# End of the attention in a two-layer cross-attention kernel: last group's sums in the score banks, transposes ahead of the picks, heads 0 and 1 mostly split beforehand

## Chip, cores and metric

One core of a Trainium2 chip. The metric is the device time of one execution in microseconds, as the median of several. TensorE is PE in the profile, VectorE DVE, ScalarE ACT, GpSimd POOL, SyncE SP.

## What is computed

Two cross-attention layers and an MLP, in float32, on x of 8 x 56 x 256 with one context of 8 x 1500 x 256:

```python
B, Q, D, H, K, T, F = 8, 56, 256, 16, 128, 1500, 1024
def cross(q_in, kv, wq, bq, wk, bk, wv, bv, wo, bo, bias_k, bias_v):
    qh = heads(q_in @ wq + bq)                     # b q h k
    kh = concat(heads(kv @ wk + bk), bias_k)       # one extra key
    vh = concat(heads(kv @ wv + bv), bias_v)       # one extra value
    w  = softmax(einsum('bqhk,bthk->bhqt', qh, kh) / sqrt(K))
    return einsum('bhqt,bthk->bqhk', w, vh).reshape(B, Q, H * K) @ wo + bo
for layer in (1, 2):
    x = x + cross(layer_norm(x), ctx, ...)
x = x + gelu(layer_norm(x) @ w_fc1 + b_fc1) @ w_fc2 + b_fc2
```

## The kernel before

**Order of the mathematics.** Keys and values are never formed. The queries of each head are carried through the head's key weights, so that scores are products with the raw context, and the attention weights multiply the raw context as well. The sum, 256 wide for each of the 8 x 56 x 16 = 7168 rows, is then taken through the value weights and the output weights of its head. The extra key and value come in separately: a column of logits `lb`, its softmax share `pn_extra`, and a product with the row `dv80`.

**Precision.** Each operand is split in two float32r parts, HI (rounded) and LO (the rest), and a product is three matmuls, HI HI, HI LO and LO HI. ACT or VectorE makes HI, VectorE or GpSimd makes LO.

**Attention loop.** A batch has 7 tiles of 128 rows (16 heads times 8 queries each), in two groups of GT = 4 and 3 tiles. A group takes NCT = 12 chunks of 125 context positions. TensorE computes a chunk's scores in one of two score banks (0 and 1, `S_BANK`), ACT copies them to `slots`, VectorE keeps the running maximum. 14 steps later (`SUB_LAG`) VectorE subtracts the maximum (L1142), ACT writes the exponential's HI part in the ring `pt` and again its full value (L893, L894) and GpSimd the LO part (L486); 17 steps later (`PV_LAG`) TensorE multiplies with the context (`weighted_context`, L642 to L644: three matmuls for each tile, 9 for a chunk of the second group) in banks 2 to 5 (`O_BANK`).

**Closing a group.** `normalized`: VectorE forms the denominators and reciprocals (L1177, L1180), ACT scales tiles 0 and 2 (L900), VectorE tile 1 and 3 (L1184) and the extra share (L1186). TensorE transposes `on` into bank 7 (L653) in two goes, and ACT copies each to `qt` (L907), the second go after the first copy. All this normally lies inside the next group's steps.

**The end of a layer**, `batch_steps(B, False, True)`, has no scores any more: 17 steps of lagging work. Then, on TensorE: the 16 picks (L811, which gather `pn_extra` by head in bank 6), the transposes of the last group, and head 0. Each head has these steps: ACT gathers its rows of `qt` as HI (`context_hi`, L954), VectorE the LO part (`context_lo`, L1222); TensorE multiplies with the value weights, six matmuls (L591), and adds `dv80` times `pm` (L666), where `pm` is the picked share times a mask (GpSimd, `mask_extra`, L545); ACT adds the bias and splits off HI (L959), VectorE LO (L1228); TensorE adds the head's output rows (L675, 12 matmuls) in four banks, two heads behind. Weights of the heads are loaded by SyncE in four staging tiles, split by ACT (HI, `weight_hi`, L840) and GpSimd (LO, `weight_lo`, L427); a staging tile is loaded anew after its LO part is done.

**What sets the order.** Every engine's order is written by hand and runs strictly as written; engines wait on counting semaphores. Before the change, of the second weights' first four tiles ACT splits two within the last steps (k = 11 and 13) and two after the picks' copy (L942); GpSimd takes two LO parts at its steps 12 and 13, waits for the last context matmul, makes `dv80` (L531, L534), then the other two LO parts, then `pm` for heads 0 and 1. ACT's order after the last scaled copy is: `p80` (picks), two weights, two transposed copies, then heads 0 and 1. VectorE's is: LO part of the picks (L1233), `context_lo` of heads 0 and 1.

Buffers share space: `w` and `w_raw` lie over the first group's `slots`, `cs`, `pm` and `dv80` over the second's, `oth` (the gathered heads) over the scaled queries `qs`.

## Time and profile before

| | us |
|---|---|
| median of 3 runs | 1302.52 |
| lowest, highest | 1300.93, 1304.53 |
| the profiled execution, its own time | 1303.02 |
| its span in the profile | 1301.2 |
| TensorE busy in the span | 1245.8 (96%) |
| VectorE, ACT, GpSimd busy | 795.3, 806.5, 902.6 |

The busy time of an engine counts its instructions, not waits on semaphores. A row of the timeline is one instruction or a run of like ones, with its start, its duration, and in brackets how long the engine had been idle before it and which operation released it. Matmuls overlap each other, so that rows of 0.28 us start 0.12 us apart. "Granted clock" is TensorE's clock as a share of 2.4 GHz, at either 1.0 or 0.5; values between them are means over a window.

### The profile page before, as it was taken

How to read it: one execution, taken by the hardware profiler on the slowest of the kernel's cores; microseconds unless marked ns; L12 is line 12 of the kernel's file. 1: busy time of each engine (PE TensorE's matmuls, PEld its weight loads, DVE VectorE, ACT ScalarE, POOL GpSimd, SP SyncE). 2: the span in 40 equal slices, each digit the busy share in tenths (PEclk: the TensorE clock that was granted, in tenths of full speed). 3: DMA queues.
4: the chain of work that ended last, by engine and by line, in shares of the span. 5: the costliest groups of instructions: out<-in, count | busy, mean ns of one | idle time of the engine just before them, and what ended most of it. 6: DMA issues, size and time to landing. Idle time of an engine off the chain costs nothing.

```text
span 1301.2 us, 27136 instructions
## 1 busy us (share of the span) xinstructions
PE 1245.8 (96%) x8016; PEld 1144.4 (88%) x8016; DVE 795.3 (61%) x1368; ACT 806.5 (62%) x1572; POOL 902.6 (69%) x750
## 2 busy tenths in 40 slices
PE   6999999999999999989699999999999999999887
PEld 5779999999999998978686999999999999999787
DVE  6855666666666666537684666666656666664554
ACT  4745666666666666666384666666666666667554
POOL 4737777777777686667572768686868786867772
PEclk9999999999999999999899999999999999999898
DMA  5401111111111111122251111111111111101231
GB/s 174 130 9 48 37 60 37 57 43 59 49 50 47 47 47 35 36 59 64 80 165 36 37 36 60 35 59 38 56 45 61 36 59 35 59 24 45 57 90 31
DMA packets 30426, 72.69 MB, mean 56 GB/s; under 512 B 3072, under 2 KB 4144, under 8 KB 30368
## 3 DMA queue, kind: packets, MB, share of 16 engines
q1 hardware_dynamic: 30368, 72.01, 18.0%
q8 instruction: 25, 0.41, 0.1%
q14 instruction: 33, 0.27, 0.1%
HBM read 71.52 MB, written 0.48 MB: 55 GB/s over the span
## 4 chain that ended last, share of the span: by engine, by line
PE 85%; DVE 5%; ACT 3%; issue 3%; DMA 1%; POOL 1%; DVEq 0%; ACTq 0%; POOLq 0%; SPq 0%
PE psum L621 34%; PE psum L642 13%; PE psum L644 12%; PE psum L643 12%; PE psum L591 5%; PE psum L675 4%; PE psum L653 2%; DVE g_prod L1091 1%; PE psum L628 1%; PE psum L635 1%; PE psum L612 1%; ACT slots L925 1%; DMA w_raw<-weights 1%; DVE t_max L1154 1%; PE psum L666 1%
## 5 line engine op out<-in xcount | busy, mean ns | idle before, releaser
L486 POOL TENSOR_TENSOR pt<-slots,pt 125x512 fp32r<-125x512 f32 (+1 forms) x384 | 444.6, 1162 | 217.7 <-ACT slots L894 185.3
L621 PE MATMUL psum<-qs,ctx 128*125 128x384 f32 (+1 forms) x2304 | 540.9, 371 | 4.7 <-DVE qs L1131 2.4
L621 PEld LDWEIGHTS psum<-qs,ctx 128*125 128x125 f32 x2304 | 394.4, 186 | 50.6 <-ACT slots L925 9.5
L642 PE MATMUL psum<-ctx,pt 125*128 125x258 f32 x1344 | 385.8, 287 | 5.2 <-ACT on L900 4.2
L643 PE MATMUL psum<-ctx,pt 125*128 125x256 f32 x1344 | 379.3, 282 | 0.0
L644 PE MATMUL psum<-ctx,pt 125*128 125x258 f32 x1344 | 379.2, 282 | 0.0
L1154 DVE TENSOR_TENSOR t_max<-psum,t_max 125x512 f32<-125x512 f32 (+1 forms) x320 | 199.5, 623 | 261.8 <-PE psum L621 261.2
L893 ACT ACTIVATE pt<-slots 125x512 fp32r<-125x512 f32 (+1 forms) x384 | 221.7, 577 | 191.7 <-DVE slots L1142 178.3
L925 ACT ACTIVATE slots<-psum 125x512 f32<-125x512 f32 (+1 forms) x384 | 207.5, 541 | 145.4 <-DVE t_max L1154 135.0
L642 PEld LDWEIGHTS psum<-ctx,pt 125*128 125x128 f32 x1344 | 253.6, 189 | 22.8 <-ACT on L900 14.7
L643 PEld LDWEIGHTS psum<-ctx,pt 125*128 125x128 f32 x1344 | 254.1, 189 | 6.0
L644 PEld LDWEIGHTS psum<-ctx,pt 125*128 125x128 f32 x1344 | 254.7, 189 | 0.0
L1142 DVE TENSOR_TENSOR slots<-slots,psum 125x512 f32<-125x512 f32 (+1 forms) x384 | 233.3, 612 | 17.9 <-PE psum L635 17.7
L894 ACT ACTIVATE slots<-slots 125x512 f32<-125x512 f32 (+1 forms) x384 | 217.2, 566 | 0.0
L427 POOL TENSOR_TENSOR w<-w_raw,w 128x512 fp32r<-128x512 f32 x72 | 106.8, 1488 | 68.7 <-ACT w L840 66.1
L436 POOL TENSOR_TENSOR ctx<-nat_stage,ctx 125x768 fp32r<-125x768 f32 (+1 forms) x64 | 113.2, 1769 | 14.9 <-DVE ctx L1048 14.6
L443 POOL TENSOR_TENSOR ctx<-tr_stage,ctx 128x750 fp32r<-128x750 f32 (+1 forms) x64 | 106.8, 1669 | 21.8 <-DVE ctx L1054 21.8
L451 POOL TENSOR_TENSOR qs<-qt,qs 128x384 fp32r<-128x384 f32 (+1 forms) x60 | 68.8, 1147 | 11.1 <-POOL qs L448 11.1
L1054 DVE CAST ctx<-tr_stage 128x750 fp32r<-128x750 f32 (+1 forms) x64 | 70.8, 1107 | 0.8 <-DMA tr_stage<-ctx_tr 0.8
L591 PE MATMUL psum<-ht,w 128*128 128x448 f32 x240 | 63.3, 407 | 6.6 <-issue 3.5
L1048 DVE CAST ctx<-nat_stage 125x768 fp32r<-125x768 f32 (+1 forms) x64 | 60.5, 945 | 3.7 <-DMA nat_stage<-ctx_nat 3.6
L675 PE MATMUL psum<-w,cs 128*112 128x256 f32 x480 | 62.4, 281 | 0.0
(84 smaller groups left out, 1045.5 us busy)
## 6 DMA issues: line engine op xcount, KB each, us to landing
nat_stage<-ctx_nat SPq DMA_DIRECT2D x64, 375.0 KB
tr_stage<-ctx_tr SPq DMA_DIRECT2D x64, 375.0 KB, 3.1
w_raw<-weights SPq DMA_DIRECT2D x72, 256.0 KB, 2.7
dk_all<-dk_rows SPq DMA_DIRECT2D x2, 768.0 KB, 6.5
dk_all<-dk_rows SPq DMA_DIRECT2D x2, 256.0 KB, 3.8
xres<-x_rows SPq DMA_DIRECT2D x4, 112.0 KB, 2.2
out_rows<-xres SPq DMA_DIRECT2D x4, 112.0 KB, 2.0
bo<-out_bias SPq DMA_DIRECT2D x1, 336.0 KB, 3.8
```

The costliest lines, as they stand in the source:

```text
L486: nc.gpsimd.tensor_tensor(split_weights(h, LO, c), slot(h, c), as_f32(split_weights(h, HI, c)), ALU.subtract).then_inc(pt_lo, 1)
L591: last = mm(out_bank, w[u][:, a, c * P:(c + 1) * P], moving(m, c), start=(m, c, a) == (HI, 0, HI), stop=(not more and (m, c) == (LO, DC - 1)))
L621: last = mm(scores(h, k), ctx_tr_chunk(half, a, c), qs[h][:, m, half, 0:R], start=(half, a, m) == terms[0], stop=(half, a, m) == terms[-1])
L642: mm(O_BANK[j][:, 0:D + 2], hi, ctx_nat_hi(c), start=(c == 0), stop=False, skip_group_check=True)
L643: mm(O_BANK[j][:, 0:D], hi, ctx_nat_lo(c), start=False, stop=False, skip_group_check=True)
L644: return mm(O_BANK[j][:, 0:D + 2], lo, ctx_nat_hi(c), start=False, stop=(c == NCT - 1), skip_group_check=True)
L675: last = mm(Y_BANK[g][0:RGP, 0:D], cs[u][:, a, rows], w[u][:, m, D:2 * D], start=first and (a, m) == (HI, HI), stop=last_head and (a, m) = ...
L893: go(split_weights(h, HI, c), slot(h, c), ACT.Exp)
L894: go(slot(h, c), slot(h, c), ACT.Exp).then_inc(exp_done, 1)
L925: go(slot(h, c), scores(h, k), ACT.Copy).then_inc(copied, 1)
L1142: V.tensor_tensor(slot(h, c), slot(h, c), shift(h), ALU.subtract).then_inc(sub_done, 1)
L1154: V.tensor_tensor(t_max[h][:], scores(h, k), before, ALU.max).then_inc(max_done, 1)
```

## The change

Five edits, in each of the two layers.

1. The second group of the last batch sums its three tiles in banks 0, 1 and 2 (`O_LAST`) rather than 2, 3 and 4. Banks 0 and 1 wait for nothing but the last score copy, bank 2 for the scaled copy of the group before.
2. TensorE transposes the last group's tiles right after its sums, tiles 0 and 1 to bank 7 and tile 2 to bank 5 (`OT_LAST`), and picks after that. ACT copies bank 7, VectorE bank 5.
3. ACT writes 53 of the 56 row tiles (`EARLY`) of heads 0 and 1 before the last group is closed, and the last three when it is; VectorE does so for the LO part of head 0. Head 1's LO part stays whole.
4. ACT splits one weight tile within the last steps rather than two, and the three others after its early copies, ahead of the last scaled copies. GpSimd splits none there; it makes `dv80` right after the last LO part of the attention weights and then splits all four.
5. TensorE runs the six value matmuls of both heads 0 and 1 first (`first_contexts`) and the two matmuls with `pm` after them. The LO part of the picks comes behind head 1's LO part on VectorE.

```diff
+EARLY = NT - GT[1]
...
         O_BANK = [bank[2 + j] for j in range(GT[0])]
+        O_LAST = [bank[j] for j in range(GT[1])]
         NB_BANK, MT_BANK, OT_BANK = bank[6], bank[7], bank[7]
+        OT_LAST = bank[5]
...
                     weights_lo(B, i, h, c)
-                    if k in (12, 13):
-                        weight_lo(l * JOBS + (H + k - 12), k - 12)
-
-                pool.wait_ge(pv_mm, INIT + (l + 1) * LAYER_STEPS)
+
+                pool.wait_ge(pt_lo, INIT + (l + 1) * LAYER_STEPS)
...
-                for u in range(2, 4):
+                for u in range(4):
                     weight_lo(l * JOBS + (H + u), u)
...
+            def first_contexts(n, job):
+
+                for u in range(2):
+                    pe.wait_ge(w_lo, INIT + job + u + 1)
+                    pe.wait_ge(c_lo, INIT + n + u - 3)
+                    project(C_BANK[u][:, 0:ROWS], u, lambda m, c, u=u: oth[u][:, m, c, :],
+                            ((oth_hi, INIT + n + u + 1, 0), (oth_lo, INIT + n + u + 1, 0)), True)
+                for u in range(2):
+                    pe.wait_ge(pm_ready, INIT + n + u + 1)
+                    mm(C_BANK[u][:, 0:ROWS], dv80[:], pm[u][:], start=False, stop=True).then_inc(c_mm, 1)
...
                     for j in range(GT[h]):
-                        if c == 0 and j in (0, 2):
+                        if c == 0 and out_banks is O_LAST and j < 2:
+                            pe.wait_ge(copied, INIT + (l + 1) * LAYER_STEPS)
+                        elif c == 0 and out_banks is O_LAST:
+                            pe.wait_ge(on_act, INIT + (l + 1) * (2 * GROUPS) - 3)
+                        elif c == 0 and j in (0, 2):
                             pe.wait_ge(on_act, INIT + l * (2 * GROUPS) + b * 4 + (i // NCT) * 2 + j // 2 - 1)
-                        if c == 0 and j == 1:
+                        elif c == 0 and j == 1:
                             pe.wait_ge(on_dve, INIT + l * (3 * B) + b * 3 + (i // STEPS) * 3 + h)
-                        last = weighted_context(h, c, j)
+                        last = weighted_context(h, c, j, out_banks[j])
...
+                            group_contexts(b, i, ph, pc, O_LAST if tail and ph else O_BANK)
...
+                pe.wait_ge(on_act, INIT + (l + 1) * (2 * GROUPS) - 1)
+                pe.wait_ge(on_dve, INIT + (l + 1) * (3 * B))
+                context_transposes(0, 2, OT_BANK)
+                pe.wait_ge(on_act, INIT + (l + 1) * (2 * GROUPS))
+                context_transposes(2, GT[1], OT_LAST)
+
                 pe.wait_ge(pn_ready, INIT + (l + 1) * GROUPS)
                 settle(pe)
-
                 for j in range(TQ):
                     last = mm(PICK_BANK[0:EXTRA, j * NT:(j + 1) * NT], pick[:, j, :], pn_extra[:],
                               start=(j == 0), stop=True, skip_group_check=True)
                 last.then_inc(pn_picked, 1)
-                group_transposes(B - 1, 1, 0, OT_BANK)
-                group_transposes(B - 1, 1, 1, OT_BANK)
-
                 heads, jobs = l * H, l * JOBS + H
-                for u in range(2):
-                    head_context(u, heads + u, jobs + u, True)
+                first_contexts(heads, jobs)
                 output_quad(heads, jobs, True, True, False)
...
-                        if tail and k in (11, 13):
-                            u = (k - 11) // 2
-                            weight_hi(l * JOBS + (H + u), u, l * 8 + 4)
+                        if tail and k == 11:
+                            weight_hi(l * JOBS + H, 0, l * 8 + 4)
...
-                normalized(B - 1, 1)
+                act.wait_ge(ot_out, INIT + (l + 1) * (2 * GROUPS) - 2)
+                for s in range(2):
+                    go(by_tile(oth[s][:, HI])[:, :, 0:EARLY], head_rows_of(s)[:, :, 0:EARLY],
+                       ACT.Copy).then_inc(oth_early, 1)
+                for u in range(1, 4):
+                    weight_hi(l * JOBS + (H + u), u, l * 8 + 4)
+                normalized(B - 1, 1, O_LAST)
+                act.wait_ge(ot_mm, INIT + (l + 1) * (2 * GROUPS) - 1)
+                go(qt_flat[:, :, B * FLAT - GT[1] * P:B * FLAT - (GT[1] - 2) * P],
+                   OT_BANK[:, 0:DC * 2 * P].rearrange("p (c r) -> p c r", c=DC), ACT.Copy).then_inc(ot_out, 2)
+                act.wait_ge(ot_out, INIT + (l + 1) * (2 * GROUPS))
+                act.wait_ge(ot_last, INIT + l + 1)
+                for s in range(2):
+                    go(by_tile(oth[s][:, HI])[:, :, EARLY:NT], head_rows_of(s)[:, :, EARLY:NT],
+                       ACT.Copy).then_inc(oth_hi, 1)
                 act.wait_ge(pn_picked, INIT + l + 1)
                 go(p80[:].rearrange("p (t e) -> p t e", e=TQ), PICK_BANK[0:EXTRA, 0:ROWS].rearrange(
                     "p (e t) -> p t e", e=TQ), ACT.Copy).then_inc(p80_hi, 1)
-                for u in range(2, 4):
-                    weight_hi(l * JOBS + (H + u), u, l * 8 + 4)
-                transposed_context(B - 1, 1, 0)
-                transposed_context(B - 1, 1, 1)
-                act.wait_ge(ot_out, INIT + (l + 1) * (2 * GROUPS))
...
-                for s in range(2):
-                    context_hi(s, s, l * H)
...
-                normalized(B - 1, 1)
+                def early_lo(s):
+
+                    dve.wait_ge(oth_early, INIT + l * 2 + s + 1)
+                    V.tensor_tensor(by_tile(oth[s][:, LO])[:, :, 0:EARLY], head_rows_of(s)[:, :, 0:EARLY],
+                                    by_tile(as_f32(oth[s][:, HI]))[:, :, 0:EARLY], ALU.subtract)
+
+                early_lo(0)
+                normalized(B - 1, 1, O_LAST)
+                dve.wait_ge(ot_mm, INIT + (l + 1) * (2 * GROUPS))
+                V.tensor_copy(qt_flat[:, :, B * FLAT - P:B * FLAT],
+                              OT_LAST[:, 0:DC * P].rearrange("p (c r) -> p c r", c=DC)).then_inc(ot_last, 1)
+                dve.wait_ge(oth_hi, INIT + l * H + 1)
+                V.tensor_tensor(by_tile(oth[0][:, LO])[:, :, EARLY:NT], head_rows_of(0)[:, :, EARLY:NT],
+                                by_tile(as_f32(oth[0][:, HI]))[:, :, EARLY:NT], ALU.subtract).then_inc(oth_lo, 1)
 
...
+                context_lo(1, 1)
                 dve.wait_ge(p80_hi, INIT + l + 1)
                 p80_l = p80[64:EXTRA].rearrange("p (t e) -> p t e", e=TQ)
                 V.tensor_tensor(p80_l, PICK_BANK[64:EXTRA, 0:ROWS].rearrange("p (e t) -> p t e", e=TQ),
                                 as_f32(p80_l), ALU.subtract).then_inc(p80_lo, 1)
-                for s in range(2):
-                    context_lo(s, s)
```

The denominators are read from `O_LAST` as well, and two new counters, `ot_last` and `oth_early`, go with it.

## Rows read from the trace of the kernel before

**Rows 1.** The page of the kernel before: busy time by engine, first line.

```profile
PE 1245.8 (96%) x8016; PEld 1144.4 (88%) x8016; DVE 795.3 (61%) x1368; ACT 806.5 (62%) x1572; POOL 902.6 (69%) x750
```

**Rows 2.** Timeline, TensorE, end of layer 1: start us, us, operation, count [idle before].

```profile
562.26 0.39 PE L642 MATMUL psum<-ctx,pt 125*128 125x258 f32 x1 [0.98 <-ACT on L900]
...
575.77 0.39 PE L642 MATMUL psum<-ctx,pt 125*128 125x258 f32 x1 [0.46 <-POOL pt L486]
...
576.84 0.28 PE L644 MATMUL psum<-ctx,pt 125*128 125x258 f32 x1
...
578.55 1.32 PE L811 MATMUL psum<-pn_extra,pick 128*80 128x56 f32 x16 [1.44 <-DVE pn_extra L1186]
...
582.03 0.44 PE L653 MATMUL psum<-ident,on 128*128 128x128 f32 x2 [1.70 <-ACT qt L907]
...
584.10 2.58 PE L591 MATMUL psum<-oth,w 128*128 128x448 f32 x6 [1.63 <-ACT oth L954]
...
586.47 0.57 PE L666 MATMUL psum<-pm,dv 80*128 80x448 f32 x1
...
591.21 1.57 PE L675 MATMUL psum<-w,cs 128*112 128x256 f32 x12
```

**Rows 3.** The same of GpSimd.

```profile
573.48 1.28 POOL L427 TENSOR_TENSOR w<-w_raw,w 128x512 fp32r<-128x512 f32 x1
...
574.72 0.99 POOL L486 TENSOR_TENSOR pt<-slots,pt 125x384 fp32r<-125x384 f32 x1
...
577.39 0.29 POOL L531 CAST dv<-dv 80x128 fp32r x1 [0.43 <-PE psum L644]
577.94 0.45 POOL L534 TENSOR_TENSOR dv<-dv,dv 32x128 fp32r<-32x128 f32 x1 [0.26 <-POOL dv L531]
...
581.15 2.49 POOL L427 TENSOR_TENSOR w<-w_raw,w 128x512 fp32r<-128x512 f32 x2 [2.76 <-ACT w L840]
...
583.60 2.67 POOL L545 TENSOR_TENSOR pm<-p,mask 80x448 fp32r<-80x448 f32 x2
```

**Rows 4.** The same of ACT.

```profile
561.74 0.84 ACT L900 ACTIVATE on<-psum,rden 128x256 f32<-128x256 f32 x2 [0.85 <-DVE rden L1180]
...
573.06 0.62 ACT L840 ACTIVATE w<-w_raw 128x512 fp32r<-128x512 f32 x1
...
577.56 0.84 ACT L900 ACTIVATE on<-psum,rden 128x256 f32<-128x256 f32 x2 [3.89 <-DVE rden L1180]
...
581.39 0.58 ACT L907 ACTIVATE qt<-psum 128x512 f32<-128x512 f32 x1
...
583.00 1.79 ACT L954 ACTIVATE oth<-qt 128x896 fp32r<-128x896 f32 x2
```

**Rows 5.** Windows: length, busy us of PE, PEld, DVE, ACT, POOL, granted clock, DMA.

```profile
584.00:591.00 7.00, 6.91 (x20) 6.09 (x21) 5.11 (x5) 3.17 (x5) 4.13 (x4) 0.56 0.23 64
591.00:606.00 15.00, 14.50 (x94) 12.99 (x93) 12.75 (x16) 10.43 (x16) 12.21 (x8) 1.00 0.20 55
...
640.00:660.00 20.00, 15.14 (x63) 13.63 (x64) 12.15 (x26) 9.39 (x17) 4.89 (x5) 0.71 0.33 98
...
1209.00:1216.00 7.00, 3.28 (x24) 2.67 (x25) 1.80 (x3) 4.48 (x8) 4.24 (x5) 0.67 0.30 77
```

**Rows 6.** Timeline of layer 2: VectorE's last sum, TensorE's first output rows.

```profile
1207.99 0.16 DVE L1177 TENSOR_TENSOR den<-psum,p_extra 128x3 f32<-128x3 f32 x1 [10.21 <-PE psum L644]
...
1221.65 1.57 PE L675 MATMUL psum<-w,cs 128*112 128x256 f32 x12
```

**Rows 7.** Timeline, VectorE, layer 1.

```profile
577.16 0.16 DVE L1177 TENSOR_TENSOR den<-psum,p_extra 128x3 f32<-128x3 f32 x1 [10.20 <-PE psum L644]
...
580.49 0.62 DVE L1233 TENSOR_TENSOR p<-psum,p 16x448 fp32r<-16x448 f32 x1 [2.08 <-ACT p L942]
...
588.70 1.09 DVE L1222 TENSOR_TENSOR oth<-qt,oth 128x896 fp32r<-128x896 f32 x1
...
596.66 2.47 DVE L1222 TENSOR_TENSOR oth<-qt,oth 128x896 fp32r<-128x896 f32 x1
```

More of the change, by code:

```diff
@@ L894, in weights_hi, with normalized @@
                     go(slot(h, c), slot(h, c), ACT.Exp).then_inc(exp_done, 1)
-                def normalized(b, h):
+                def normalized(b, h, out_banks):
                     act.wait_ge(rden_ready, INIT + l * GROUPS + b * 2 + (h + 1))
                     for j in range(0, GT[h], 2):
-                        go(on[:, j], O_BANK[j][:, 0:D], ACT.Copy,
+                        go(on[:, j], out_banks[j][:, 0:D], ACT.Copy,
                            scale=rden[:, ds(b * TILES + (h * GT[0] + j), 1)]).then_inc(on_act, 1)
@@ L915, in batch_steps @@
                         if c == 5 and not first:
-                            normalized(b - 1, h)
+                            normalized(b - 1, h, O_BANK)
                         i, ph, pc = lagging(k, SUB_LAG)
```

29 lines of the change are left out of this document (15 added, 14 removed).

## The prediction

> **What bounds the kernel now.** I read the page first: TensorE is busy for 96% of the span [rows 1], so a change pays only where TensorE waits, or where its clock is low. The diff touches the end of each layer's attention, so I then read the timeline of every engine from the last chunks of the weighted context to the first output rows. The reader is to see three things there.
>
> First, before the last context matmul TensorE has two small holes: 0.98 us before the last group's first chunk (released by the scaled copy at L900, which empties the bank that is written again) and 0.46 us before its last chunk (released by the last low half from GpSimd) [rows 2]. That low half ran at 574.72 because GpSimd had put a weight subtraction of 1.28 us in front of it at 573.48 [rows 3].
>
> Second, from the last context matmul (it starts at 576.84 and lasts 0.28, so it ends at 577.12; call that T0) TensorE does little for 7.0 us: picks, four transposes, a wait of 1.70 us for the ACT copy that empties their bank, two transposes, a wait of 1.63 us for the head's high half [rows 2]. On ACT the two head copies start at 583.00, behind two weight copies and the bank copy of 581.39 [rows 4]. The first mask product, which head 0 needs for its last matmul, starts at 583.60 behind two weight subtractions [rows 3].
>
> Third, the price shows at the first output rows (L675): they start at 591.21, T0 + 14.1 us [rows 2]. From there TensorE is the limit again: 14.50 us busy of 15 [rows 5]. In layer 2 the end of the contexts is at 1207.95 (VectorE's sum starts at 1207.99, 0.04 after its input, as in layer 1) and the output rows start at 1221.65, T0 + 13.7 us [rows 6, 7]. Those 14 us hold some real TensorE work, the picks, transposes and three heads; the rest is waiting, and whatever the start of L675 gains is passed on, since all that follows is driven by TensorE.
>
> The granted clock belongs to this: 0.56 from 584 to 591, that is 2 x 0.44 x 7 = 6.2 us at the lower of the two levels (1.2 GHz, the higher is 2.4), and 0.67 from 1209 to 1216 in layer 2, 4.6 us [rows 5]. It fell after TensorE had done little since T0.
>
> **The change, part by part.**
>
> Banks. The last group's tiles 0 and 1 go to the score banks, free since the last score was copied; only tile 2 waits, for the first L900 copy. That copy ends near 561.74 + 0.42 = 562.16 [rows 4], and TensorE is ready at 562.26 - 0.98 = 561.3 [rows 2]. Six matmuls fit (a chunk of nine takes 1.07 us at 0.12 apart), so chunk 0 ends near 562.6 and not 563.4: 0.7 us.
>
> No weight subtraction before the last low half. It runs at 573.48 to 574.47 (0.99) [rows 3], and the 0.46 us hole with its restart goes: 0.6 us. Both together would give 1.3, but the low half now ends only 0.1 ahead of its use; 574.6 + 8 x 0.12 + 0.28 puts the new T0 at 575.85. Gain 1.25 us. If the low halves turn out to feed TensorE more slowly, only some 0.4 us is left; that is the bound below, 1.6 (both holes and their restarts) the one above.
>
> ACT after its last exponential. The weight copy of 573.06 [rows 4] leaves that place; two early head copies of 53 of 56 tiles come instead. The whole copies take 1.79 for two [rows 4], so these 1.7 us, to 574.8. Three weight copies at up to 0.62 (they overlap a little) follow, to about 576.5. The reciprocal will be there at T0 + 0.40 = 576.25, as 577.56 against 577.16 shows [rows 4, 7], so ACT comes 0.25 us late to it. That is the price of putting three weight copies ahead, and I count it. The two scaled copies end at 576.95 and 577.35.
>
> TensorE. Four transposes start at 577.0 (0.6 us; two took 0.44, so 0.9 at most), two more follow the second copy, in another bank, until 577.85, and the 16 picks of 1.32 us [rows 2] end at 579.05. The picks are now behind the transposes: they start 1.9 us after T0 instead of 1.4. They hide the ACT copy out of the first bank (0.58, to 578.3), VectorE's copy of the second (0.4 to 0.5, the rate of L900), and two tiny late copies of three tiles. Their size is in no row; 0.16 for a tiny operation [rows 7] is the bound below and a whole copy of 0.94 above; I take 0.2, because 48 elements are nearer to the tiny one. Head 0's matmuls start at 579.05, T0' + 3.2 where they started T0 + 7.0.
>
> VectorE. The early low half of head 0 (1.03) lies beside idle time, before T0'. After the tiny late part comes all of head 1's low half, from 578.9. Alone this operation takes 1.09, beside GpSimd up to 2.47 [rows 7]; I take 1.8, between them because GpSimd will be in its weight subtractions all that time: 580.7. The picks' low half (0.62) [rows 7] is queued behind it and ends at 581.3. Head 1's matmuls, at 0.2 each, wait for its low half and end near 581.3 too.
>
> GpSimd. From the last low half at 574.5: the two small value operations take 1.0 (577.39 to 578.39) [rows 3], four weight subtractions 4 x 1.28 = 5.1, to 580.6. VectorE's operations push them by 1.1 (one whole operation) to 2.0; I take 1.4, 582.0. The first mask product (2.67 for two beside VectorE, so 0.9 to 1.3) lands at 583.1. **This is the new late comer**: both heads wait for it with one matmul each (0.37 to 0.57), and all later heads are queued behind. Head 0 is complete at 583.5, against 587.04.
>
> From there to L675 it takes: cs copy and gaps 0.9, head 2's high copy 0.94, its low half 1.09, two matmuls and the value term 0.6, that is 3.5 to 3.6; the interval of before, 587.04 to 591.21 = 4.2 with the low clock in it, is the bound above. L675 starts at 587.1, T0' + 11.25. The weight loads for heads 4 to 7 now leave 2 to 3 us later for heads 4 and 5, since their staging tiles come free later; ACT takes these up only after the first output rows, near 588, and the later ones are issued by 582: what hides them is 6 us and more, and if that cover were gone each us of lateness would be one of TensorE's.
>
> **Sum.** Layer 1: 591.2 - 587.1 = 4.1 us. Layer 2: T0' = 1206.7, L675 at 1217.95 instead of 1221.65: 3.7 us. Together 7.8 us. The profiled execution took 1303.0 (span 1301.2); it becomes 1295.2. It stood 0.5 above the median, so the median becomes 1294.7. With the ends of the unknowns a layer gains between 2 and 5 us: 4 to 10 us in all.
>
> One rule speaks against the order chosen. The row shows a low half of 2.47 us where the same one alone took 1.09 [rows 7]. The Trainium skill (SBUF — State Buffer, Who interferes with whom) says why such a thing may be: a VectorE instruction with two SBUF inputs and a GpSimd instruction that reads SBUF block each other for a whole instruction, whichever comes first. By that rule the early low half could also hold up the last low half of the attention weights, if it starts first.
>
> **The rivals.**
>
> (A) Blocking between VectorE and GpSimd costs more. If the early low half comes before the last attention low half, T0' moves by 1.0 us; if head 1's low half then waits the full 1.4 us [rows 7] and the mask product with it, a layer gains 4 - 1 - 1 = about 2: 1298.7. For it: the 2.47 of the trace. Against: ACT's early copy ends at about 574.0, when GpSimd is in its last operation already.
>
> (B) The clock. If it falls while heads 2 and 3 and the first output rows run, low time costs half of itself where TensorE is the limit. 3 us of it per layer costs 1.5: 1297.7. It is also the case **on the other side**: the gain of 3.9 us per layer is gone once the low clock covers 7.8 us of TensorE-bound output work per layer; at the start of the next stage it did last 2 x 0.29 x 20 = 11.6 us [rows 5]. With that in both layers the kernel is 2 x (5.8 - 3.9) = 3.8 slower: 1306.3. Against: both low stretches at the place in question held 6 to 7 us, and mostly lay over waiting; and TensorE is to wait less than before.
>
> (C) The work is hidden anyway: the mask product lands no earlier than before, so L675 moves by T0's 1.25 alone and less. 1300 to 1302. Against: its two inputs come about 1 to 2 us earlier, and the weight subtractions before it start 5 us earlier.
>
> (D) More than thought: no blocking and no low clock (in layer 1 it now covers the matmuls of heads 0 and 1). 5.3 us per layer, 1292.
>
> **How the numbers follow.** Forecast 0.58 (1293 to 1297.5), A 0.12, B as a mere loss 0.08, C 0.07, D 0.11, B with its sign turned 0.04. A measurement of this kernel can tell about 0.3%, 3.9 us, from no change; the three times shown are 3.6 us apart, so I add about 1.5 us on each side. Range 1290.5 to 1299.5. Faster by over 0.3%: forecast, D, A and B, less what lies at 1298.6 and above, 0.86; within: 0.10; slower 0.04.
>
> **What would show it.** Last context matmul 1.0 to 1.5 us earlier, without the two holes. First matmul of head 0 about 3 us after it; first mask product 7 to 8 us after it, released by its queue and not by the picks; L675 about 11 us after it in both layers. The forecast is wrong if L675 comes later than T0' + 13, if the weight operations of ACT delay the scaled copies by over 0.5 us, or if the granted clock is near 0.5 while L675 runs.

## The result, and the profile after

The changed kernel took 1298.22 us in the median of 9 executions (1294.46 to 1300.98) against 1303.45 (1300.56 to 1305.23) for the kernel before, run beside it. The ratio is 0.9956 with a 95% interval of 0.9943 to 0.9970, that is 5.7 us faster, between 3.9 and 7.4. Run once more, in the first group of experiments, it had 0.9971 (0.9957 to 0.9985), 3.8 us. Forecast were 1294.7 us and a gain of 7.8: direction and range held, and the gain forecast was 2 to 4 us too large. The second median, 1299.69 us, lies 0.2 us above the forecast range. The ratios leave out an execution that stands far above all others of its kernel; below that was one, of 1517.44 us, in experiment 12.

The profiled execution was the slowest of the nine, 1300.98 us. TensorE's timeline at the end of layer 1 answers to [rows 2]; L643 to L645 are the context matmuls, L592 the head matmuls, L681 the value terms of heads 0 and 1, L687 the output rows.

```profile
561.64 0.39 PE L643 MATMUL psum<-ctx,pt 125*128 125x258 f32 x1 [0.26 <-ACT on L917]
...
575.00 0.28 PE L645 MATMUL psum<-ctx,pt 125*128 125x258 f32 x1
576.36 0.88 PE L654 MATMUL psum<-ident,on 128*128 128x128 f32 x6 [1.08 <-DVE on L1208]
577.08 1.29 PE L832 MATMUL psum<-pn_extra,pick 128*80 128x56 f32 x16
578.18 2.59 PE L592 MATMUL psum<-oth,w 128*128 128x448 f32 x10
581.41 0.68 PE L592 MATMUL psum<-oth,w 128*128 128x448 f32 x2 [0.63 <-DVE oth L1259]
583.26 0.47 PE L681 MATMUL psum<-pm,dv 80*128 80x448 f32 x1 [1.17 <-POOL pm L546]
584.15 0.74 PE L681 MATMUL psum<-pm,dv 80*128 80x448 f32 x1 [0.42 <-POOL pm L546]
585.48 2.64 PE L592 MATMUL psum<-oth,w 128*128 128x448 f32 x6 [0.59 <-ACT oth L978]
587.92 0.57 PE L667 MATMUL psum<-pm,dv 80*128 80x448 f32 x1
588.29 2.72 PE L687 MATMUL psum<-w,cs 128*112 128x256 f32 x12
```

The contexts end at 575.00 + 0.28 = 575.28 (T0'). The first hole is 0.26 us instead of 0.98, the second is gone. The heads' matmuls start 2.9 us after T0' instead of 7.0. But then come four new holes, 0.63, 1.17, 0.42 and 0.59 us, each with little work between them, and the row at 588.29 takes 2.72 us where the one of [rows 2] took 1.57. ACT, answering to [rows 4]:

```profile
571.96 1.71 ACT L958 ACTIVATE oth<-qt 128x848 fp32r<-128x848 f32 x2
573.57 1.66 ACT L857 ACTIVATE w<-w_raw 128x512 fp32r<-128x512 f32 x3
575.73 0.84 ACT L917 ACTIVATE on<-psum,rden 128x256 f32<-128x256 f32 x2 [0.50 <-DVE rden L1204]
...
577.80 0.38 ACT L969 ACTIVATE oth<-qt 128x48 fp32r<-128x48 f32 x2
578.40 0.54 ACT L972 ACTIVATE p<-psum 80x448 fp32r<-80x448 f32 x1 [0.23 <-PE psum L832]
```

The early copies, the three weight splits and the late copies of 0.19 us each come in the order forecast. From T0' the early copies end 0.6 us and the weight splits 0.7 us sooner than forecast (T0' - 1.6 and - 0.05); the scaled copies start 0.45 us after T0', as before (0.44). VectorE, answering to [rows 7], then GpSimd, answering to [rows 3]:

```profile
572.89 1.40 DVE L1245 TENSOR_TENSOR oth<-qt,oth 128x848 fp32r<-128x848 f32 x1 [6.55 <-ACT oth L958]
...
578.07 1.16 DVE L1254 TENSOR_TENSOR oth<-qt,oth 128x48 fp32r<-128x48 f32 x1 [0.37 <-ACT oth L969]
579.15 2.20 DVE L1259 TENSOR_TENSOR oth<-qt,oth 128x896 fp32r<-128x896 f32 x1
581.38 0.62 DVE L1271 TENSOR_TENSOR p<-psum,p 16x448 fp32r<-16x448 f32 x1
...
585.37 1.58 DVE L1259 TENSOR_TENSOR oth<-qt,oth 128x896 fp32r<-128x896 f32 x1
```

```profile
573.66 0.78 POOL L532 CAST dv<-dv 80x128 fp32r x1 [0.27 <-POOL pt L489]
...
575.42 4.99 POOL L430 TENSOR_TENSOR w<-w_raw,w 128x512 fp32r<-128x512 f32 x4 [0.25 <-ACT w L857]
582.27 3.73 POOL L546 TENSOR_TENSOR pm<-p,mask 80x448 fp32r<-80x448 f32 x4 [1.87 <-DVE p L1271]
```

GpSimd runs four weight subtractions without a gap from 575.42 to 580.41, and then idles for 1.87 us until the picks' low half is there. VectorE's operation on 48 elements per partition (the tiny late low half of head 0) took 1.16 us, and the whole low half of head 1 after it 2.20, where it takes 1.09 alone. The cast of GpSimd at 573.66, beside VectorE's early low half, took 0.78 us, against 0.29 before [rows 3]. The granted clock, answering to [rows 5]:

```profile
583.00:592.00 9.00, 7.73 (x27) 6.40 (x28) 6.79 (x10) 4.94 (x7) 3.06 (x5) 0.62 0.00 1
1214.00:1223.00 9.00, 7.46 (x26) 6.30 (x27) 6.67 (x10) 4.95 (x7) 3.04 (x5) 0.62 0.03 9
```

0.62 over 9 us is 6.8 us at the lower level, in both layers. In layer 1 it lasted from 584.0 to 590.8. So it now lies over head 2, the first output rows and head 3, and not over heads 0 and 1. Last, the layer's last 36 output matmuls:

```profile
628.15 4.39 PE L687 MATMUL psum<-w,cs 128*112 128x256 f32 x36
```

The start of this "last group", and of the first 12 output matmuls (the "first rows"), both measured from the end of the contexts, are how I compare kernels below, since an execution drifts by 1 to 3 us before it gets there. The last group was at T0 + 53.4 and 52.8 us in the two layers of the kernel before and is at T0' + 52.9 and 53.0. All such places and all lengths of a low clock below are of one execution per kernel.

### The profile page after: what moved, and what is told of

Its sections match the earlier page's. It is cut to its first block, busy times and chain, and to the rows that moved or that the text cites. A ratio compares the mean times of both kernels' runs of the same rounds, so it can differ in the third digit from the quotient of the medians.

```text
span 1299.2 us, 27148 instructions
## 1 busy us (share of the span) xinstructions
PE 1249.0 (96%) x8016; PEld 1146.3 (88%) x8016; DVE 797.1 (61%) x1372; ACT 804.8 (62%) x1574; POOL 898.8 (69%) x750
## 4 chain that ended last, share of the span: by engine, by line
PE 86%; DVE 5%; issue 3%; ACT 2%; DMA 2%; POOL 1%; DVEq 0%; SPq 0%; ACTq 0%; POOLq 0%
PE psum L622 35%; PE psum L643 13%; PE psum L645 12%; PE psum L644 12%; PE psum L592 4%; PE psum L687 4%; DMA w_raw<-weights 2%; PE psum L654 2%; PE psum L636 1%; PE psum L629 1%; DVE g_prod L1113 1%; ACT on L917 1%; PE psum L667 0%; PE psum L613 0%; PE psum L578 0%
## 5 line engine op out<-in xcount | busy, mean ns | idle before, releaser
L643 PE MATMUL psum<-ctx,pt 125*128 125x258 f32 x1344 | 385.7, 287 | 2.8 <-ACT on L917 2.7
L645 PE MATMUL psum<-ctx,pt 125*128 125x258 f32 x1344 | 379.3, 282 | 0.0
L643 PEld LDWEIGHTS psum<-ctx,pt 125*128 125x128 f32 x1344 | 253.6, 189 | 20.3 <-ACT on L917 13.2
L645 PEld LDWEIGHTS psum<-ctx,pt 125*128 125x128 f32 x1344 | 254.7, 189 | 0.0
L439 POOL TENSOR_TENSOR ctx<-nat_stage,ctx 125x768 fp32r<-125x768 f32 (+1 forms) x64 | 113.5, 1774 | 14.7 <-DVE ctx L1070 14.0
L592 PE MATMUL psum<-ht,w 128*128 128x448 f32 x240 | 61.7, 399 | 5.9 <-issue 3.1
L687 PE MATMUL psum<-w,cs 128*112 128x256 f32 x480 | 64.7, 288 | 0.0
L687 PEld LDWEIGHTS psum<-w,cs 128*112 128x112 f32 x480 | 63.1, 182 | 1.7
```

Of the source, the lines that this page charges most:

```text
L592: last = mm(out_bank, w[u][:, a, c * P:(c + 1) * P], moving(m, c), start=(m, c, a) == (HI, 0, HI), stop=(not more and (m, c) == (LO, DC - 1)))
L643: mm(out_bank[:, 0:D + 2], hi, ctx_nat_hi(c), start=(c == 0), stop=False, skip_group_check=True)
L645: return mm(out_bank[:, 0:D + 2], lo, ctx_nat_hi(c), start=False, stop=(c == NCT - 1), skip_group_check=True)
L687: last = mm(Y_BANK[g][0:RGP, 0:D], cs[u][:, a, rows], w[u][:, m, D:2 * D], start=first and (a, m) == (HI, HI), stop=last_head and (a, m) = ...
```

## The experiments

Here T0' stands for the end of the contexts in every kernel that has the change, T0 in the others. The mask product is GpSimd's `pm`, and the picks' low half on VectorE is its input. Two theories. **Clock**: what the gain lacks is lost since the low clock now lies over work that nothing hides. **Blocking**: it is lost between VectorE and GpSimd, which hold each other up, so that the mask product is late. The rivals in the single runs are named in their expectations.

**1. The same kernel again.**

> The changed kernel once more, nothing edited. Theory 1 (the clock decides what is left of the gain): the end of the contexts and the first output rows stand 13.0 us apart again within 0.3 us, since all of it is fixed order, but the low stretch of TensorE's clock may lie elsewhere, and the whole time moves with the mean granted clock (the nine runs so far: 1294.5 at 0.987, 1301.0 at 0.980). Theory 2 (the low stretch always lies over the first output rows): the row L687 takes 2.7 us again in both layers. Time 1295 to 1300.

1299.69 us (1295.03 to 1303.98, 12 executions). From T0', first output rows at 12.86 us in both layers, last group at 52.2. The steps up to the value terms are the same to 0.03 us as in the first trace, but the low clock was shorter. Windows of this execution:

```profile
583.00:592.00 9.00, 6.47 (x25) 4.73 (x26) 6.32 (x11) 4.34 (x7) 3.60 (x4) 0.81 0.14 44
1214.00:1223.00 9.00, 7.97 (x41) 6.93 (x41) 7.34 (x11) 5.82 (x10) 3.60 (x4) 0.81 0.00 1
```

0.81 over 9 us is 3.4 us at the lower level instead of 6.8, and the first output rows took 2.18 and 2.22 us. So the order is fixed and the clock is what varies. The 12 times go with the mean granted clock: 1295.0 at 0.987, 1304.0 at 0.980. It was neither 2.7 us in both layers nor a low clock elsewhere: it touched the first output rows in both traces, for a varying part.

**2. Holes filled**, to test the clock.

```diff
+                def keep_busy(times):
+                    for _ in range(times):
+                        mm(bank[1][0:CT, 0:ROWS], ctx_tr_chunk(0, HI, 0), ctx[:, 0:ROWS], start=True, stop=True,
+                           skip_group_check=True)
...
+                keep_busy(5)
                 for u in range(2):
                     pe.wait_ge(pm_ready, INIT + n + u + 1)
                     mm(C_BANK[u][:, 0:ROWS], dv80[:], pm[u][:], start=False, stop=True).then_inc(c_mm, 1)
+                    keep_busy(2 + u)
```

> The changed kernel with 5, 2 and 3 extra matmuls of 448 columns (into a bank nobody reads) in the three holes around the value terms of heads 0 and 1; nothing else is moved. Theory 1 (the gain fell short by the low clock over head 2 and the first output rows): the granted clock stays at 1.0 from the picks on, head 2's six matmuls take 1.4 instead of 2.6 us and the first output rows 1.6 instead of 2.7; 2 to 2.5 us per layer, so 4 to 5 us under the changed kernel, near 1293. Rival (blocking between VectorE and GpSimd is the whole shortfall, the clock no matter): no gain, or up to 1 us slower by the extra matmuls.

1295.76 us (1294.37 to 1299.38), ratio 0.9944 (0.9926 to 0.9962). Timeline of TensorE (L677 are the extra matmuls, L695 the output rows) and windows:

```profile
583.25 0.67 PE L592 MATMUL psum<-oth,w 128*128 128x448 f32 x2 [0.63 <-DVE oth L1267]
583.76 1.18 PE L677 MATMUL psum<-ctx 128*125 128x448 f32 x5
585.10 0.47 PE L688 MATMUL psum<-pm,dv 80*128 80x448 f32 x1 [0.16 <-POOL pm L546]
...
587.33 1.05 PE L592 MATMUL psum<-oth,w 128*128 128x448 f32 x4 [0.25 <-ACT oth L986]
...
589.45 1.59 PE L695 MATMUL psum<-w,cs 128*112 128x256 f32 x12
```

```profile
583.00:592.00 9.00, 7.97 (x39) 6.19 (x40) 6.28 (x11) 4.84 (x7) 3.68 (x5) 1.00 0.16 51
1214.00:1223.00 9.00, 8.65 (x57) 7.83 (x56) 9.00 (x12) 5.90 (x10) 5.19 (x4) 1.00 0.10 29
```

The clock stays at 1.00. Head 2's matmuls are 1.05 + 0.67 us instead of 2.64, the output rows 1.59 instead of 2.72. First rows at T0' + 12.31, last group at 51.43 in both layers, so 1.4 and 1.6 us better than the first trace and 0.8 than the second. The clock theory holds, at about half the size that I gave it: the low halves still set most of head 2's time, which a faster TensorE can't shorten. In the median it is 2.5 to 3.9 us; against the changed kernel of the same group, by the two ratios, 3.5 us, with intervals that still overlap a little (0.9926 to 0.9962 and 0.9957 to 0.9985).

**3. The picks' low half ahead of head 1's**, to move the mask product.

```diff
-                context_lo(1, 1)
                 dve.wait_ge(p80_hi, INIT + l + 1)
...
                                 as_f32(p80_l), ALU.subtract).then_inc(p80_lo, 1)
+                context_lo(1, 1)
```

> The changed kernel with the picks' low half (L1271) ahead of head 1's low half on VectorE. If the mask product is late only because its input waits behind head 1's low half (2.20 us), it now starts when GpSimd's four weight subtractions end, 1.9 us earlier, while the first value term comes 1 us earlier, since it stands behind head 1's matmuls, whose low half is 0.6 us later: 0.5 to 1.1 us per layer, 1 to 2 us in all. If blocking by GpSimd moves with it, head 1's low half takes over 2 us again and the gain is 0 to 1 us.

1298.29 us (1295.08 to 1299.65), ratio 0.9957 (0.9941 to 0.9973). Of this execution VectorE, GpSimd and the windows of both layers:

```profile
581.37 0.62 DVE L1270 TENSOR_TENSOR p<-psum,p 16x448 fp32r<-16x448 f32 x1
582.02 1.45 DVE L1259 TENSOR_TENSOR oth<-qt,oth 128x896 fp32r<-128x896 f32 x1
```

```profile
577.53 4.99 POOL L430 TENSOR_TENSOR w<-w_raw,w 128x512 fp32r<-128x512 f32 x4 [0.25 <-ACT w L857]
582.47 4.47 POOL L546 TENSOR_TENSOR pm<-p,mask 80x448 fp32r<-80x448 f32 x4
```

```profile
584.00:593.00 9.00, 7.60 (x26) 6.33 (x26) 6.67 (x10) 4.94 (x7) 3.04 (x5) 0.62 0.09 29
1213.00:1222.00 9.00, 7.87 (x28) 6.62 (x29) 6.68 (x10) 4.94 (x7) 3.04 (x4) 0.62 0.07 24
```

The mask products now start when the weight subtractions end. The first output rows came at T0' + 11.87, 1.0 to 1.1 us earlier than in both traces of the changed kernel, as forecast. The last group stood at 52.2 and 51.9. How much of the gain that is depends on the trace it is held against: 0.7 and 1.1 us against the first, which had 6.8 us of low clock in each layer as this one has, but only 0.0 and 0.3 us against the second, which had 3.4. The first rows again took 2.76 us, and the second 12 output matmuls came at 16.3 and 16.0, against 17.0 and 17.1 in the first trace and 16.3 in the second. So what the mask product wins is lost in part in the low clock right behind it, and the time can't be told from the changed kernel's.

**4. Two weight subtractions behind the mask products**, to test blocking.

```diff
-                for u in range(4):
+                for u in range(2):
                     weight_lo(l * JOBS + (H + u), u)
...
                 for s in range(2):
                     mask_extra(s, s, l * H)
+                for u in range(2, 4):
+                    weight_lo(l * JOBS + (H + u), u)
```

> The changed kernel with GpSimd's weight subtractions 2 and 3 behind the mask products of heads 0 and 1 instead of ahead of them. Theory (blocking: VectorE's tiny low half of 1.16 us and head 1's of 2.20 us wait for GpSimd's weight subtractions): the tiny one takes 0.2 us, head 1's 1.1, the first mask product starts 2 us earlier (near 5 us after the end of the contexts instead of 7.0), and the first output rows 1.5 to 2.5 us earlier; 3 to 5 us in all, near 1294. Rival (head 2's weights are now what is late): the first output rows move by less than 0.7 us and the time is the same within 1.5 us.

1297.07 us (1296.38 to 1298.32), ratio 0.9951 (0.9936 to 0.9967), 2.6 us under the changed kernel of the same group, with intervals that overlap. VectorE:

```profile
578.87 0.21 DVE L1256 TENSOR_TENSOR oth<-qt,oth 128x48 fp32r<-128x48 f32 x1 [0.37 <-ACT oth L971]
579.00 1.09 DVE L1261 TENSOR_TENSOR oth<-qt,oth 128x896 fp32r<-128x896 f32 x1
580.12 0.62 DVE L1273 TENSOR_TENSOR p<-psum,p 16x448 fp32r<-16x448 f32 x1
...
584.11 2.15 DVE L1261 TENSOR_TENSOR oth<-qt,oth 128x896 fp32r<-128x896 f32 x1
```

The same 48-element operation takes 0.21 us and head 1's low half 1.09, with GpSimd idle beside them; in the changed kernel they took 1.16 and 2.20. So blocking is shown, worth 2.06 us on VectorE. In the changed kernel the third of the four subtractions ends at about 575.42 + 3 x 1.25 = 579.17 and the tiny low half at 579.23; the fourth ends at 580.41, and head 1's low half 0.94 us later. Each of VectorE's operations waits for the end of the subtraction beside it. The value terms come at T0' + 5.92 instead of 7.98. It did not all arrive, for GpSimd's two subtractions now meet head 2's low half (2.15 us at 584.11), and the clock is low. TensorE:

```profile
584.22 1.28 PE L594 MATMUL psum<-oth,w 128*128 128x448 f32 x4 [0.86 <-ACT oth L980]
586.31 1.11 PE L594 MATMUL psum<-oth,w 128*128 128x448 f32 x2 [0.81 <-DVE oth L1261]
587.22 0.62 PE L669 MATMUL psum<-pm,dv 80*128 80x448 f32 x1
587.64 2.76 PE L689 MATMUL psum<-w,cs 128*112 128x256 f32 x12
```

```profile
584.00:593.00 9.00, 7.97 (x32) 6.77 (x33) 7.63 (x10) 3.91 (x7) 6.54 (x6) 0.62 0.19 58
```

First rows at T0' + 11.57, 1.3 to 1.4 us earlier; last group at 52.15 and 51.93. The low clock lasted 6.8 us in each layer here too, so this is 0.7 and 1.1 us earlier than in the first trace of the changed kernel, with the same low clock, and 0.0 and 0.3 us earlier than in the second, with half of it. The first rows moved by a little less than the 1.5 to 2.5 expected and by far more than the rival's 0.7, and again only a part of it reached the layer's end.

The Trainium skill says of this (SBUF — State Buffer, Who interferes with whom) that a VectorE instruction with two SBUF inputs and a GpSimd instruction that reads SBUF block each other for the whole instruction. The traces agree: 1.16 us against 0.21 for the smallest of them. The picks' low half has only one input in SBUF, the other is in PSUM: it took 0.62 us in experiment 3, where the fourth weight subtraction (the row of 4.99 us, until 582.52) ran beside it, and 0.62 with GpSimd idle. GpSimd's four mask products took 4.47 us in experiment 3, where head 1's low half ran beside the first, and 3.73 in the changed kernel.

**5 to 7. The end of the contexts by parts.** One execution each, of 1301.56, 1303.42 and 1301.10 us, too few to tell times apart; only the place of the contexts' end is read. First edit 1 of the change alone, then GpSimd's subtractions alone, then both; everything else as in the kernel before.

```diff
-                            group_contexts(b, i, ph, pc)
+                            group_contexts(b, i, ph, pc, O_LAST if tail and ph else O_BANK)
```

```diff
-                    if k in (12, 13):
-                        weight_lo(l * JOBS + (H + k - 12), k - 12)
...
-                for u in range(2, 4):
+                for u in range(4):
                     weight_lo(l * JOBS + (H + u), u)
```

> The kernel before with only the first edit: the last group's tiles 0 and 1 are summed in the score banks. Read in one trace as the distance from the denominators of the group before (L1177, 128x4) to the end of the contexts, 15.80 us before and 14.58 in the changed kernel. Theory (GpSimd's weight subtraction in front of the last low half holds the end): the first hole is gone, but the last low half still lands where it did, so the distance is 15.7 to 15.8. Rival (the first hole is what was won): 14.9 to 15.2.

> The kernel before with only GpSimd's weight subtractions 0 and 1 moved out of the last steps, behind its value operations. Same distance. Theory: the second hole of 0.46 us and its restart go, the first stays: 15.1 to 15.3. Rival (only both together free anything): 15.7 and more.

> Both of these on the kernel before, nothing else of the change: the distance is that of the changed kernel, 14.6, if these two edits are all that moved the end of the contexts; near 14.9 if taking ACT's second weight split out of the steps has a part in it.

Distance from the denominators of the group before to the end of the contexts, in layers 1 and 2: before 15.80 and 15.81; banks 15.32 and 15.29; subtractions 15.04 in both; both 14.57 in both; the changed kernel 14.58 in both. Banks alone and subtractions alone:

```profile
562.96 0.39 PE L643 MATMUL psum<-ctx,pt 125*128 125x258 f32 x1 [0.26 <-ACT on L905]
...
575.99 0.39 PE L643 MATMUL psum<-ctx,pt 125*128 125x258 f32 x1 [0.46 <-POOL pt L487]
```

```profile
563.99 0.39 PE L640 MATMUL psum<-ctx,pt 125*128 125x258 f32 x1 [0.98 <-ACT on L898]
```

My theory for the banks missed, and the rival's 14.9 to 15.2 was just missed as well: they gave 0.5 us by themselves, with the hole of 0.46 us before the last chunk still there. The last low half had moved along: it started 12.92 us after the same denominators instead of 13.40. ACT's wait of 0.35 us for TensorE's transposes in between is gone in this trace; that this is the reason isn't shown. The parts, 0.50 and 0.76, are together 1.26, about the whole, 1.23. So the two edits account for all of the contexts' gain.

In the last of these three kernels the output rows start 13.6 and 13.7 us after the contexts, against 14.1 and 13.7 before. With the banks alone they started at 14.7 in layer 1 and 13.7 in layer 2; in layer 1 the low clock had lasted 10.2 us there, from 1.3 us after the contexts on, and in layer 2 6.8 us.

**8. The kernel before, holes filled**, in the three holes of [rows 2].

```diff
+                keep_busy(5)
                 pe.wait_ge(pn_ready, INIT + (l + 1) * GROUPS)
...
                 group_transposes(B - 1, 1, 0, OT_BANK)
+                keep_busy(7)
                 group_transposes(B - 1, 1, 1, OT_BANK)
+                keep_busy(7)
```

> The kernel before with 5, 7 and 7 extra matmuls of 448 columns in the three holes after the contexts, to keep TensorE's clock up there. Theory 1 (in the kernel before the low clock lay over heads 0 and 1 and cost part of the 14 us): the clock stays at 1.0, the first output rows start 12.3 to 13.2 us after the end of the contexts instead of 13.7 and 14.1, and the time falls by 1 to 3 us, to about 1301. The change then is worth the difference of the two filled kernels, about 5 us, and not 7.8. Rival (it lay over waits for the low halves only and cost nothing): within 0.5 us of the kernel before, 1303.

1301.75 us (1296.47 to 1303.39), ratio 0.9983 (0.9968 to 0.9998). The clock is at 1.00 in both layers' windows, the first output rows start at T0 + 12.85 and 12.86, the last group at 51.95 and 51.98. So the low clock cost the kernel before 0.8 to 1.2 us per layer up to its output rows; it lay over waits for the most part, as the forecast had it, but not wholly. The two filled kernels compared: 51.95 against 51.43. **At full clock, all of the change behind the contexts is worth 0.5 us per layer**, and the contexts' own 1.2. By these traces that is 3.5 us in all; the two ratios, 0.9944 against 0.9983, say 5.1, with 2.0 and 2.3 us of uncertainty (together 3.1), so 3.5 is within it. The two kernels have their extra matmuls in different holes.

**9. Both cures together**: experiment 4's edit, and matmuls in the holes it leaves.

```diff
+                keep_busy(2)
                 for u in range(2):
                     pe.wait_ge(pm_ready, INIT + n + u + 1)
                     mm(C_BANK[u][:, 0:ROWS], dv80[:], pm[u][:], start=False, stop=True).then_inc(c_mm, 1)
+                    keep_busy(2 + 2 * u)
```

> Two weight subtractions behind the mask products, and 2, 2 and 4 extra matmuls in the holes around the value terms. Theory (blocking and the low clock are two separate losses): the first output rows start 11.0 to 11.3 us after the end of the contexts as in the kernel with the two subtractions moved (11.57, with the clock low), and from there the output stage takes its 39.1 us at full clock, so the layer's last row group starts at 50.2 to 50.6 instead of 52.2 (changed kernel) and 51.4 (filled); 1 us per layer under the filled kernel, near 1294. Rival (once the clock is up, head 3 or the low halves hold the first quad): 51.2 to 51.5, the time of the filled kernel.

1295.69 us (1294.30 to 1297.10, 5 executions), ratio 0.9937 (0.9923 to 0.9951). TensorE (L697 are the output rows) and windows; T0' is 576.00:

```profile
587.37 1.59 PE L697 MATMUL psum<-w,cs 128*112 128x256 f32 x12
```

```profile
583.00:592.00 9.00, 7.76 (x45) 6.40 (x45) 8.64 (x10) 5.81 (x10) 7.90 (x6) 1.00 0.18 59
```

First rows at T0' + 11.37 (a little outside the 11.0 to 11.3 expected: head 2's low half is the blocked one), last group at 50.5 in both layers, as forecast: 0.9 us under the filled kernel per layer. This is the best of all kernels run by its ratio, though its median is that of the filled kernel (1295.76); the 1.9 us between them are in the traces and not resolved in the times. Against the medians of the changed kernel it is 2.5 to 4.0 us faster. Against the kernel before, the layers end 2.9 and 2.3 us earlier behind the contexts and 1.2 us each before them: 7.6 us by the traces, 8.2 (6.4 to 10.0) by the ratio. That is the gain forecast for the change, 7.8, and the first rows stand within 0.1 us of the forecast T0' + 11.25. So the clock and the blocking account for what the forecast lacked, as far as one execution shows it.

**10. Without the early copies**, on ACT and, alike, on VectorE (edit 3 undone).

```diff
-                for s in range(2):
-                    go(by_tile(oth[s][:, HI])[:, :, 0:EARLY], head_rows_of(s)[:, :, 0:EARLY],
-                       ACT.Copy).then_inc(oth_early, 1)
...
                 for s in range(2):
-                    go(by_tile(oth[s][:, HI])[:, :, EARLY:NT], head_rows_of(s)[:, :, EARLY:NT],
-                       ACT.Copy).then_inc(oth_hi, 1)
+                    go(by_tile(oth[s][:, HI]), head_rows_of(s), ACT.Copy).then_inc(oth_hi, 1)
```

> The changed kernel without its third edit: ACT copies heads 0 and 1 whole after the last group is closed, VectorE makes head 0's low half there too. By the rows (0.94 for a whole copy against 0.19, 1.09 to 2.20 for a whole low half against 1.13 for the blocked tiny one) the picks reach VectorE 1.5 us later: first output rows 14.0 to 14.8 us after the end of the contexts against 12.9. If it is 13.0 or less, the early copies bought nothing because the tiny late ones wait as long.

First rows at T0' + 13.37 and 13.38, with head 2 at the low clock (2.51 us): 0.4 to 0.5 us later than the changed kernel, not 1.1 to 1.9. Last group at 52.4 and 52.5, 0.2 to 0.3 us later than in the second trace of the changed kernel, which had as much low clock (3.4 us in each layer). The time of its one execution was 1298.21. The early copies bought 0.4 us at the first rows. Without them VectorE's low halves took 2.00 and 1.08 us and ended at T0' + 6.55, with them 1.16 and 2.20 and 6.07: GpSimd's weight subtractions, over at T0' + 4.6 and 5.1, are in the way of both orders. Without the early low half beside it, GpSimd's cast takes 0.29 us again instead of 0.78, and the subtractions start and end 0.5 us earlier: that is the price of the early low half.

**11. Picks ahead of the transposes** (edit 2's order undone).

```diff
-                context_transposes(0, 2, OT_BANK)
-                pe.wait_ge(on_act, INIT + (l + 1) * (2 * GROUPS))
-                context_transposes(2, GT[1], OT_LAST)
...
                 last.then_inc(pn_picked, 1)
+                context_transposes(0, 2, OT_BANK)
+                pe.wait_ge(on_act, INIT + (l + 1) * (2 * GROUPS))
+                context_transposes(2, GT[1], OT_LAST)
```

> The changed kernel with the picks ahead of the transposes again, all else as changed. The head copies then wait for transposes that end 1.3 us later, and the picks come 0.4 us earlier; ACT takes the picks after the head copies either way, so the mask product comes 1.0 to 1.3 us later: first output rows at 13.9 to 14.2 us after the end of the contexts. Rival (GpSimd's queue and blocking hide the order): 12.9 to 13.1.

First rows at T0' + 12.40 and 12.38, last group at 51.5, no low clock at either layer's end, time of the one execution 1297.15. I expected 1.0 to 1.3 us of loss; against the filled kernel, which is at full clock too, it lost 0.1. The rival had foreseen no loss, but at the low clock (12.9 to 13.1). VectorE shows why:

```profile
579.85 0.76 DVE L1253 TENSOR_TENSOR oth<-qt,oth 128x48 fp32r<-128x48 f32 x1 [0.37 <-ACT oth L968]
580.53 1.08 DVE L1258 TENSOR_TENSOR oth<-qt,oth 128x896 fp32r<-128x896 f32 x1
581.64 0.62 DVE L1270 TENSOR_TENSOR p<-psum,p 16x448 fp32r<-16x448 f32 x1
```

T0' is 575.46 here. The tiny low half comes 1.6 us later than in the changed kernel and ends at T0' + 5.15, where GpSimd's four subtractions end (5.08); head 1's then takes 1.08 us and ends at 6.15, where it ended at 6.07 in the changed kernel. In both orders GpSimd's queue sets the end of the low halves.

**12. The same, timed**, for the clock had stayed up by itself in experiment 11.

> The kernel of the last experiment again, now timed. In its one execution the first output rows started at 12.4 us after the end of the contexts at full clock, though the transposes come later than in the changed kernel. Theory (its holes before the mask products are shorter, so the low clock stays away in every execution, without extra matmuls): first output rows at 12.4 again, the layer's last row group at 51.5, and a time of 1295 to 1297.5, at or under the changed kernel (1298.2 and 1299.7) and near the filled one (1295.8). Rival (chance of one execution): the low clock comes back over head 2 in this trace or in most executions, and the median is 1298 to 1300.

The ratio is 0.9958 (0.9942 to 0.9974), the median 1298.47 (seven executions, six of them between 1296.80 and 1300.70): the changed kernel's. In this trace the first rows of layer 1 started at T0' + 12.54 and took

```profile
590.21 2.76 PE L687 MATMUL psum<-w,cs 128*112 128x256 f32 x12
```

so the low clock came back, for 3.4 us in each layer. The full clock of experiment 11 was chance. The rival won: transposes first or picks first, the times can't be told apart.

This also bears on experiment 2, for one execution at full clock shows little. Over all traces: of the 22 layer ends without extra matmuls a low stretch began in 20 between the end of the contexts and the first rows (in all but the two of experiment 11), of the 6 with them in none.

## Why the prediction was right, and where it was off

Direction and range held. The case that I called the forecast (1293 to 1297.5) did not come: 1298.22 lies between rival B's 1297.7 and rival A's 1298.7. Two of the three signs of being wrong came true. The granted clock was at the lower level while the first output rows ran, and these rows started at T0' + 13.01 in layer 1 of the first trace, where 13 was the limit (12.93, 12.86 and 12.85 in the three others). So the part up to the first head matmul was understood, and what lay behind it was not; that the time still fell into the range is owed to its width, and in part to luck, since two errors on GpSimd's path ran against each other, as told below.

- **End of the contexts**: 1.25 us forecast, 1.22 and 1.23 measured (distance to the denominators before). Banks 0.7 forecast, 0.5 measured; subtraction 0.6 forecast, 0.76 measured.
- **ACT's queue**: forecast 0.25 us late to the reciprocal for the weight splits ahead of it, measured not late at all (575.73, T0' + 0.45, against T0 + 0.44). The weight splits had ended at 575.23, before the reciprocal.
- **First head matmul**: T0' + 3.2 forecast, 2.9 measured. The late copies were taken at 0.2 us and took 0.19.
- **VectorE's low halves**: the step that was mis-sized. I counted 0.2 us for the tiny late one, which took 1.16, and 1.8 for head 1's, which took 2.20. Together 1.4 us. I had the blocking row in hand, and applied it to the long operation only.
- **Who waits for whom**: I also let VectorE push GpSimd by 1.4 us, to T0' + 6.15. That did not come: the four subtractions took 4.99 us, twice the 2.49 of two alone [rows 3], and were over at T0' + 5.1. VectorE bore the blocking by itself. The one operation of GpSimd that was held up is one that I had counted at its old length, the cast at 573.66 (0.5 us).
- **Mask product**: forecast to land at T0' + 7.25, from GpSimd's own queue. It started at T0' + 6.99 and landed near 7.9, released by VectorE's picks and not by its queue: GpSimd had been idle for 1.87 us. That it landed only 0.7 us late is luck: the picks' low half came 1.3 us later than forecast (T0' + 6.7 instead of 5.45), but the sum had already put GpSimd back by 1.4 us, for a push that did not come. Head 0 was complete at 8.45 instead of 7.65.
- **From there to the output rows**: 3.6 us taken, at full clock; 4.56 and 4.51 measured, above the 4.2 that I gave as its bound. In it lie 2.6 us of head 2 at the low clock and a blocked low half of 1.58. Sum of the steps: T0' + 13.0 and 12.9, not 11.25.
- **"Whatever the start of L675 gains is passed on"**: this held in part only. From the first output rows to the last group it took 39.3 and 39.1 us before and 39.1 filled, but 39.9 and 40.1 in the first trace of the changed kernel (39.3 and 39.4 in the second, with half the low clock), 40.3 and 40.0 with the picks first, 40.6 and 40.4 with two weights moved. The earlier the rows start, the more of the low clock lies over them. Rival B named this, with 1.5 us per layer. Against the filled kernel it was 1.4 and 1.6 us in the first trace and 0.8 in the second, of which 0.2 to 1.0 us behind the start of the rows.

So rivals A and B, to which I gave 0.20, both came true in part. Of A the blocking of VectorE came; the later end of the contexts did not (14.58 us with the early low half, 14.57 without it).

The medians say 4 to 6 us, while the traces of the same kernels add up to 2.8 (first), 4.2 (second) and 3.5 (filled). Each trace is of one execution, and these took 1303.02 us before, 1300.98 in the first and 1298.35 in the second: 2.0 and 4.7 us, near what their traces add up to. Low stretches elsewhere differ too: all of them together last about 41 us in the trace before, 52 in the first and 38 in the second. The two filled executions are only 1.4 us apart (1297.51 and 1296.07), since the changed one reached the end of its first contexts 3.0 us later. So the difference is of the size by which executions vary; no run shows another cause.

## What to carry to other kernels

When a chain between two TensorE-bound stages is shortened, look at where its low clock will lie afterwards: over waiting it cost little here (0.8 to 1.2 us of 6.8 per layer in the kernel before), over work it costs up to half of itself (the first rows took 2.76 us instead of 1.59). A few extra matmuls in the holes kept it away here and were worth more than the whole reordering behind the contexts. Hold traces against each other only with the length of their low stretches beside them. And look at an operation's blocking by what runs beside it, not by its size: 48 elements per partition cost 0.2 or 1.2 us.

## What the runs showed of the hardware

TensorE's clock fell in the changed kernel though no hole before it was longer than 1.17 us: it fell at 584.0, after holes of 0.63 and 1.17 us and in a third of 0.42, with a short matmul group between each two. It stayed at the lower level for 6.8 us although TensorE worked almost without a pause from 585.5. With 10 extra matmuls of about 0.2 us each in these holes it did not fall in either layer, nor did it in the four layer ends of the two other kernels with extra matmuls; without them it fell in 20 of 22. The same program, with the same instruction times up to there, had a low stretch of 6.8 us in both layers of one execution and of 3.4 us in both layers of another.

Of VectorE and GpSimd: a subtraction of 48 elements per partition with both inputs in SBUF took 1.16 us while GpSimd's subtractions of 1.25 us ran back to back, and 0.21 with GpSimd idle; one of 896 took 2.20 and 1.09. GpSimd's four took 4.99 us beside them, no longer than alone. One with an input in PSUM took 0.62 us in both cases.
